# Attention's values and row sums in four column groups of 32: three passes of 256 columns a step in place of two of 512, and a pair's product in two operations

## The reference, cut to what matters

```python
xn = layernorm(x)
Q, K, V = heads(xn @ Wq + bq), heads(xn @ Wk + bk), heads(xn @ Wv + bv)
scores = Q @ K.T / sqrt(64) + where(j > i, -inf, -0.25 * log(max(i - j, 1)))
x = x + merge(softmax(scores) @ V) @ Wo + bo
x = x + layernorm(x) @ Wf + bf        # Wf: 1024 x 1024, unfolded from G1, G2
```

## Time and profile before

| what | value |
|---|---|
| median of 3 executions | 655.25 us (654.42 to 657.13) |
| profiled execution | 658.8 us |
| its span, slowest core | 657.3 us (cores 648.2 to 657.3) |
| TensorE busy | 567.5 us, 86% |
| VectorE busy | 452.8 us, 69% |
| ScalarE busy | 382.9 us, 58% |
| POOL busy | 36.1 us, 5% |

### The profile page before, as it was taken

The page is one execution under the profiler, slowest core; times in us unless marked ns, Lnnn a source line. Parts: engine busy times, 40 slices in busy tenths (PEclk is TensorE's granted clock), DMA queues, the critical chain, the costliest instruction groups (busy, mean ns, idle before and its releaser), DMA issues.

```text
span 657.3 us, 11581 instructions; the slowest of 8 cores (648.2 to 657.3 us)
## 1 busy us (share of the span) xinstructions
PE 567.5 (86%) x3584; PEld 224.2 (34%) x3584; DVE 452.8 (69%) x808; ACT 382.9 (58%) x508; POOL 36.1 (5%) x44
## 2 busy tenths in 40 slices
PE   1777877989789998996999999989999999999886
PEld 0333333333224333333333333333333333333433
DVE  5675664858788675886767576767777767767572
ACT  2533543466355866774766677756767767766221
POOL 4000000000000000000000010011010110101110
PEclk9999777989778999997999999999999999999999
DMA  8999110000101000010000009563555555555555
GB/s 205 154 163 185 65 64 1 2 1 1 65 33 33 1 1 1 1 65 32 33 1 1 1 2 176 129 112 98 129 129 129 129 129 130 129 129 129 160 96 161
DMA packets 20491, 52.71 MB, mean 80 GB/s; under 512 B 1616, under 2 KB 8784, under 8 KB 20432
## 3 DMA queue, kind: packets, MB, share of 16 engines
q0 software_dynamic: 11888, 25.17, 22.9%
q1 hardware_dynamic: 8544, 26.79, 12.3%
HBM read 51.95 MB, written 8.39 MB: 92 GB/s over the span
## 4 chain that ended last, share of the span: by engine, by line
PE 62%; DVE 12%; DMA 10%; issue 8%; ACT 7%; POOL 1%; DVEq 0%; ACTq 0%; SPq 0%; POOLq 0%
PE gp L854 13%; PE pv L936 10%; PE stP L916 9%; PE pr L940 7%; PE gp L864 7%; DMA Wq<-wq 6%; PE gp L892 6%; PE gp L902 5%; ACT PT L794 5%; DVE stat L532 2%; DVE PT L671 2%; DVE stat L533 2%; DMA xrot<-x 2%; PE gp L842 1%; DVE V L578 1%
## 5 line engine op out<-in xcount | busy, mean ns | idle before, releaser
L794 ACT ACTIVATE PT<-stP,negc 128x1024 bf16<-128x1024 f32 (+1 forms) x320 | 300.4, 981 | 164.3 <-PE stP L918 164.1
L671 DVE TENSOR_TENSOR PT<-PT,decay 128x1024 bf16<-128x1024 bf16 (+1 forms) x320 | 187.3, 606 | 44.0 <-ACT PT L794 42.8
L936 PE MATMUL pv<-PT,V 128*64 128x512 bf16 (+1 forms) x320 | 116.8, 369 | 4.5 <-DVE PT L671 2.5
L938 PE MATMUL pv<-PT,V 128*64 128x512 bf16 (+1 forms) x320 | 117.3, 371 | 0.0
L942 PE MATMUL pr<-PT,ones 128*64 128x512 bf16 (+1 forms) x320 | 111.8, 359 | 0.0
L940 PE MATMUL pr<-PT,ones 128*64 128x512 bf16 (+1 forms) x320 | 111.7, 359 | 0.0
L916 PE MATMUL stP<-QT,KT 64*128 64x512 bf16 (+1 forms) x320 | 90.7, 357 | 8.6 <-ACT PT L794 8.5
L918 PE MATMUL stP<-QT,KT 64*128 64x512 bf16 (+1 forms) x320 | 90.9, 358 | 0.0
L854 PE MATMUL gp<-xnT,Wk 128*128 128x512 bf16 x256 | 70.6, 410 | 18.0 <-ACT KT L745 5.4
L864 PE MATMUL gp<-Wv,xnT 128*128 128x512 bf16 x256 | 69.2, 402 | 19.4 <-DVE V L578 6.9
L892 PE MATMUL gp<-Wo,attnT 128*128 128x512 bf16 x256 | 62.4, 380 | 7.1 <-DVE x L600 4.0
(11 more groups left out here) (71 smaller groups left out, 556.1 us busy)
## 6 DMA issues: line engine op xcount, KB each, us to landing
xrot<-x SPq DMA_DIRECT2D x24, 512.0 KB, 4.2
x<-bfn POOLq DMA_DIRECT2D x16, 512.0 KB, 5.6
out<-outb SPq DMA_DIRECT2D x16, 512.0 KB, 3.9
xrot<-bo POOLq DMA_DIRECT2D x12, 512.0 KB, 5.1
xfirst<-x SPq DMA_DIRECT2D x4, 512.0 KB, 7.7
Wk<-wk POOLq DMA_DIRECT2D x2, 1024.0 KB, 26.3
Wq<-wq POOLq DMA_DIRECT2D x2, 1024.0 KB, 33.7
Wv<-wv POOLq DMA_DIRECT2D x2, 1024.0 KB, 41.7
```

The source lines that it names most:

```text
L671: v.tensor_mul(pt, pt, decay[:, off + no:off + 512].unsqueeze(1).to_broadcast([128, 2, 512 - no])).then_inc(s_pm, 1)
L794: a.activation(p_tile(g, no), st_tile(g, no), AF.Exp, bias=negc[:, c * 8 + p % 2 * 4 + p // 2:][:, 0:1]).then_inc(s_exp, 1)
L936: t.matmul(pv[0:64, no:512], V[:, vo:vo + 64], PT[:, o + no:o + 512], start=first, stop=last, tile_position=(0, 0), skip_group_check=True)
L938: t.matmul(pv[64:128, no:512], V[:, vo + 64:vo + 128], PT[:, o + 512 + no:o + 1024], start=first, stop=last, tile_position=(0, 64), skip_g ...
```

## The change

`attn_v` now works in four column groups of 32. A group is (a, h): h is the head, and a the half of the queries, in blocks of 64 (each 128 queries are split into their first and second 64). Group (a, h) gives partitions 32(2a + h) to 32(2a + h) + 31. A values pass takes 32 of the head's 64 value columns (`half`), so there are two of them, to columns 0 to 255 and 256 to 511 of `pv`; the sums are one pass into columns 0 to 255 of `pr`, with 32 ones as weights. Each pass streams up to 256 columns, read from P in runs of 64. Per step there are 12 matmuls with 12 weight loads where there were 4 with 4.

`pv` thus holds, on partitions 64a + 32h + d, the values d (columns 0 to 255) and 32 + d (256 to 511) of head h for half a of the queries. `normalise` brings this into the order of `attnT` in two operations, one for each a: 64 partitions x 512 elements each, into 64 partitions of `attnT` that depend on the pair (even pairs 0 to 63, odd pairs 64 to 127). Ln and Exp run over 256 columns. The rows of Wo are put into the matching order on the host.

```diff
-        recip, _ = place("recip", 512, F32)
+        recip, _ = place("recip", 256, F32)
-        ones64, _ = place("ones64", 64, BF16)
+        ones32, _ = place("ones32", 32, BF16)
+        def p_part(g, h, a, no):
+            o = (g % 4) * 1024 + h * 512
+            return PT[:, o:o + 512].rearrange("p (m a q) -> p a m q", a=2, q=64)[:, a, no // 128:4]
...
-                v.tensor_mul(attnT[:, n * 512:(n + 1) * 512], pv[:, :], recip[:, :]).then_inc(s_attn, 1)
+                to = 64 * (n % 2)
+                for a in range(2):
+                    x = 64 * a
+                    out = attnT[to:to + 64, n // 2 * 1024:(n // 2 + 1) * 1024].rearrange(
+                        "p (d m a q) -> p a d m q", d=2, a=2, q=64)[:, a]
+                    ins = v.tensor_mul(out, pv[x:x + 64, :].rearrange("p (d m q) -> p d m q", d=2, q=64),
+                                       recip[x:x + 64, :].rearrange("p (m q) -> p m q", q=64).unsqueeze(1)
+                                       .to_broadcast([64, 2, 4, 64]))
+                ins.then_inc(s_attn, 1)
...
-            v.memset(ones64[:, :], 1.0).then_inc(s_const, 1)
+            v.memset(ones32[:, :], 1.0).then_inc(s_const, 1)
...
-                a.activation(recip[:, :], pr[:, :], AF.Ln).then_inc(s_rl, 1)
+                a.activation(recip[:, :], pr[:, 0:256], AF.Ln).then_inc(s_rl, 1)
...
-                t.matmul(pv[0:64, no:512], V[:, vo:vo + 64], PT[:, o + no:o + 512], start=first,
-                         stop=last, tile_position=(0, 0), skip_group_check=True)
-                t.matmul(pv[64:128, no:512], V[:, vo + 64:vo + 128], PT[:, o + 512 + no:o + 1024],
-                         start=first, stop=last, tile_position=(0, 64), skip_group_check=True)
-                t.matmul(pr[0:64, no:512], ones64[:, :], PT[:, o + no:o + 512], start=first,
-                         stop=last, tile_position=(0, 0), skip_group_check=True)
-                t.matmul(pr[64:128, no:512], ones64[:, :], PT[:, o + 512 + no:o + 1024], start=first,
-                         stop=last, tile_position=(0, 64), skip_group_check=True).then_inc(s_av, 1)
+                groups = [(a, h) for a in range(2) for h in range(2)]
+                for half in range(2):
+                    for a, h in groups:
+                        x = 32 * (2 * a + h)
+                        t.matmul(pv[x:x + 32, half * 256 + no // 2:(half + 1) * 256],
+                                 V[:, vo + h * 64 + half * 32:vo + h * 64 + half * 32 + 32], p_part(g, h, a, no),
+                                 start=first and half == 0, stop=last, tile_position=(0, x),
+                                 skip_group_check=True)
+                for a, h in groups:
+                    x = 32 * (2 * a + h)
+                    ins = t.matmul(pr[x:x + 32, no // 2:256], ones32[:, :], p_part(g, h, a, no),
+                                   start=first, stop=last, tile_position=(0, x), skip_group_check=True)
+                ins.then_inc(s_av, 1)
...
+    wo = np.ascontiguousarray(wo.reshape(4, 2, 2, 2, 32, D).transpose(0, 3, 1, 2, 4, 5).reshape(D, D))
```

More of the change, by code:

```diff
@@ L923, in attn_v @@
                 no = trim(c, mt)
-                o = (g % 4) * 1024
                 first, last = mt == 0, mt == 4 * c + 3
```

## The result

The changed kernel takes 665.9 us in the median of 4 runs (664.65 to 668.99) against 656.18 us: 1.016 of the kernel before, with an interval of 1.011 to 1.020. A second series gave 665.8 us and 1.014 (1.010 to 1.018). Forecast were 642.0 us, 633 to 654, with 0.16 on slower: wrong in sign. All medians and ratios leave out executions in which one die ran longer at a lower granted clock, which leaves two each for e6 and e9.

What follows compares the result with a forecast made beforehand. TensorE was taken to bound blocks 2 and 3, with stalls between. 18.3 us surfacing from the passes, less 2.6 and 2.4 for the pair's end, gave 13.3 us: 642.0 us as a median, range 633 to 654.

Steps and rivals of the forecast that it cites:

- Part 1: Values and sums passes on TensorE: three of 256 columns replace two of 512, saving 27.3 us of TensorE, 18.3 surfacing.
- Rival 1: Values and sums passes: a floor of 0.11 us for every pass however short, only 4.9 us gained, 650.4 us; chance 0.14.
- rival 3: Values passes: the four column groups don't overlap in a stream of passes; at 0.16 us each, 689 us; chance 0.12.
- What surfaces of it: Part 1's TensorE saving as shorter run time: a third in block 0, half in block 1, three quarters in blocks 2 and 3.
- Part 2: End of a pair: shorter Ln and Exp, product in two operations; costs 2.6 us by the chain and 2.4 by VectorE load.
- The chain Ln, Exp, product: Pair's hand-over: second product adds 0.60 us, shorter Ln and Exp take off 0.42; 11 of 31 hand-overs bound, 2.6 us in all.
- So the second ends 0.60 later: Two products on VectorE: second ends 0.60 us later, from the 0.60 between a product's start and the next operation's before.
- VectorE gets 32 x 0.60 = 19.3 us more: VectorE's added work from the second product of every pair, 0.60 us each; 2.4 us of it was forecast to surface.
- A fifth of 9.6 surfaces: Added VectorE time in blocks 0 and 1: 1.9 us of 9.6 lengthens the run; another 0.5 in blocks 2 and 3.
- Rival 4: Hand-over: a product reading one half of the partitions and writing the other takes twice as long, 28 us, 670; chance 0.04.
- The stalls: TensorE in blocks 2 and 3: some thirty stalls, each able to swallow the 0.2 us gained just before it, 6 us.
- Rival 2: Blocks 2 and 3: exponential, evictions and norms set the pace, waits take the saving; about 1 us left, 654; chance 0.08.

Runs made afterwards that it cites:

- e6: Changed kernel with a pair's product as one operation into a spare tile and two later VectorE copies to attnT: 0.986 of the kernel before, some 648 us.
- e9: e6 with the second norm's two small rstd activations moved behind the second exponential of their stretch on ScalarE: 0.967 of the kernel before, some 639 us.
- e5: e1 plus, behind each product, a VectorE operation of 64 x 512 elements that nothing waits for: 649.5 us, 0.987 of the kernel before.
- e1: Changed kernel with one product of 128 partitions a pair, in place, output not the layer's (timing alone): 636.4 us, 0.969 of the kernel before.
- e2: Kernel before with only the product of a pair split into two operations of 64 partitions: 689.0 us, 1.049 of the unsplit kernel.

## Why the prediction was wrong

**Part 1, the passes: right.** 0.77 us for two full steps (forecast 0.78), 0.37 for 256 and 128 columns (0.38 to 0.46). Rival 1's floor of 0.11 us a pass and rival 3 are out: passes of 64 columns are 0.03 us apart, with four matmuls in each. That is below 8 ns a matmul, so the 25 ns between matmuls of the Trainium skill ("TensorE: Matmul & The Clock Gate", the section on the 56 ns gap) doesn't hold for matmuls in different column groups. What surfaces of it was forecast at 18.3 us; the one-product kernel shows 20.0 (656.4 to 636.4 in its series), with the shorter reciprocal in it. Blocks 2 and 3 gave 14.0 us (forecast 15.2), but block 1 gave 5.0, not 2.5, and block 0 gave 6.9, not 0.6, which is more than the 2.3 us that TensorE has less to do there. So the near agreement of the total is in part luck, and what gave block 0 its gain isn't shown.

**Part 2, the end of a pair: the step that failed.** It was priced at 5.0 us, and the measured price is 29 to 32. Three things in it:
- "The chain Ln, Exp, product is 0.60 - 0.42 = 0.18 us longer." The 0.42 was taken off a chain without looking at what else stood ahead of the product. VectorE's own queue did: the second mask ended at 386.04, 0.4 us after the reciprocal. The trace of before had it already. Behind the reciprocal of rows 9, ready at 380.52, VectorE's masks ended at 380.59, and at 542.91 of rows 10 the product started 0.79 us after the reciprocal; in 7 of the 11 hand-overs counted the reciprocal was not on the chain at all. So the chain grew by the whole second operation, 0.69 us and not 0.18.
- "So the second ends 0.60 later" and "VectorE gets 32 x 0.60 = 19.3 us more": it ends 0.68 to 0.70 later in all pairs, and the operation behind it starts 0.72 to 0.73 after it. Here the rule weighed in the prediction, from the Trainium skill, "VectorE: DVE Perf Modes", section "Two Vector instructions with no wait between them", is the right one, and the trace agrees. It is worth 0.09 us a pair on the hand-over and 0.22 on VectorE, whose busy time grew by 25.3 us.
- "A fifth of 9.6 surfaces": in e5 about 12 of the 17.8 us of added VectorE time surface. VectorE at 70% and in order has little slack here, since short steps of longer chains are queued behind whatever is put in (344.23 and 355.16 above). The share of busy time doesn't tell this; the list of what stands behind the operation in its stretch does.

Together with 11 hand-overs forecast as bound (19 are, by the same measure of 0.15 us between product and matmul) this is 29 us where 5.0 were forecast: for the latency 10 to 16.3 us in place of 2.6, for the load 12 to 18 in place of 2.4. Where in these bounds each lies is an estimate, as said at e5.

**Rival 4** had the right place (the pair's hand-over, paid at some 20 pairs) and the wrong mechanism: a product is 0.69 us, not twice that. It got 0.04. It had the chain grow by 1.4 us at a hand-over, and it grows by 0.69. That its 670 us lie near the 666 measured is luck.

**The stalls.** Forecast was that each keeps the 0.2 us gained just before; the period pairs of block 3 show 0.43, both periods' gain. Rival 2, that the waits take what the passes save, isn't the account of the loss either: with one product (e1) 20 us of the saving surface.

**Left open:** how much of the load's price is the clock. The granted clock over the cores is 0.952 in the changed kernel, 0.959 in e5 and 0.968 to 0.969 in e1 and before, and two stretches at the 1.2 GHz level that the changed kernel has on core 7 and the kernel before doesn't (367.5 to 374.3 and 439.1 to 446.0) follow times in which TensorE was busy 2.53 of 4.5 and 6.40 of 9.1 us. As an estimate, what the clock withheld is (1 - 0.952) x 660.7 = 32 us in the changed kernel, 27 in e5 and 20 in e1 (spans as means over the cores), so of the 29 us it can hold at most some 12, and of e5's 12 at most some 7. No run changes the one without the other. Open, too, is how the 16.3 us divide between the wait and the longer hold on VectorE.

## What to carry to other kernels

Before a shorter operation is credited to a chain, look at the queue of the engine that comes next: if its earlier work ends at the same time or later, the gain is nothing, while an operation added there counts in full. Work that one accumulator's release waits for should be a single operation; move the rearranging behind the release, and to an engine on which nothing short is queued behind it. To price an added operation on an in-order engine, list what stands behind it in each stretch, not the engine's busy share.

## What the runs showed that I had not expected

Thirty-two operations of 0.69 us cost 32 us when the next pair waits for them (e2), a full microsecond each; of 0.67 us and with nothing waiting for them they cost 12 us (e5). On VectorE two operations of half the partitions each, one starting in the other half, held it for 1.42 us where one of all partitions held it for 0.60. And four column groups of 32 go on at 0.03 us a pass of 64 columns with four weight loads each, so a matmul with its load costs the array below 8 ns there.
